# A four-layer graph network on one core: the third layer's weight product as Strassen's seven half-size products over pairs of tiles

## The reference

```python
h = relu(layernorm(x))                     # layer 3, a graph convolution
deg = segment_sum(ones, dst) + 1           # self loops
dinv = 1 / sqrt(deg)
out = segment_sum((h @ W)[src] * (dinv[src] * dinv[dst]), dst) + b
x = x + relu(out)
h = relu(layernorm(x))                     # layer 4, attention
h = h @ W4
...
```

## Time and profile before

| | |
|---|---|
| runs | 986.07, 985.63, 986.05 us; median 986.05 |
| the profiled execution's span | 985.7 us, 0.35 below the median of the runs |
| TensorE matmul / weight load busy | 968.1 us (98%) / 805.6 us (82%) |
| VectorE / ScalarE / GpSimd busy | 664.2 (67%) / 468.8 (48%) / 138.7 us (14%) |
| layer three's product on TensorE | from 613.70 us to 723.40 us of the span |

### The profile page before, as it was taken

The page is one execution under the profiler, slowest core; times in us unless marked ns, Lnnn a source line. Parts: engine busy times, 40 slices in busy tenths (PEclk is TensorE's granted clock), DMA queues, the critical chain, the costliest instruction groups (busy, mean ns, idle before and its releaser), DMA issues.

```text
span 985.7 us, 14150 instructions
## 1 busy us (share of the span) xinstructions
PE 968.1 (98%) x5199; PEld 805.6 (82%) x5200; DVE 664.2 (67%) x1193; ACT 468.8 (48%) x719; POOL 138.7 (14%) x191
## 2 busy tenths in 40 slices
PE   4999999999999999999999999999999999999998
PEld 3888878888888888888888888888888888888887
DVE  6987798788788779378884115333346664967777
ACT  5778864554554547223335446001012232766654
POOL 3022400000000001223331000010000000333331
PEclk9999999999999999999999999999999999999999
DMA  6256490000000005543422040733232130201222
GB/s 237 104 191 228 129 268 1 1 23 0 0 21 0 0 0 118 103 147 125 141 93 65 1 172 8 280 118 107 86 128 70 69 122 1 86 20 66 85 85 81
DMA packets 26006, 88.29 MB, mean 90 GB/s; under 512 B 3384, under 2 KB 3580, under 8 KB 25808
## 3 DMA queue, kind: packets, MB, share of 16 engines
q1 hardware_dynamic: 15072, 52.82, 14.8%
q0 software_dynamic: 10880, 34.74, 11.6%
HBM read 59.23 MB, written 33.56 MB: 94 GB/s over the span
## 4 chain that ended last, share of the span: by engine, by line
PE 95%; DVE 1%; ACT 1%; POOL 1%; DMA 1%; issue 0%; SPq 0%; ACTq 0%; DVEq 0%; POOLq 0%
PE ps L615 22%; PE ps L2271 13%; PE ps L2245 11%; PE ps L2165 9%; PE ps L2166 9%; PE ps L2167 9%; PE ps L2221 5%; PE ps L2217 5%; PE ps L598 3%; PE ps L2088 2%; PE ps L2090 1%; PE ps L2089 1%; PE ps L2013 1%; PE ps L2016 1%; PE ps L2057 1%; PE ps L2282 1%
## 5 line engine op out<-in xcount | busy, mean ns | idle before, releaser
L2165 PE MATMUL ps<-g_hi,mask_hi 128*128 128x512 f32 x400 | 157.7, 394 | 0.2 <-DVE mask_lo L1628 0.2
L2167 PE MATMUL ps<-g_hi,mask_lo 128*128 128x512 f32 x400 | 155.9, 390 | 0.0
L2166 PE MATMUL ps<-g_lo,mask_hi 128*128 128x512 f32 x400 | 155.8, 389 | 0.0
L1144 ACT ACTIVATE mask<-ps,v 128x640 f32<-128x640 f32 x80 | 63.2, 793 | 95.7 <-PE ps L2167 49.1
L2271 PE MATMUL ps<-y_all,att_hi 128*128 128x512 f32 x380 | 103.6, 392 | 0.0
L2165 PEld LDWEIGHTS ps<-g_hi,mask_hi 128*128 128x128 f32 x400 | 75.1, 188 | 19.0 <-DVE mask_lo L1628 2.3
L581 ACT ACTIVATE hT_hi<-ps 128x1024 fp32r<-128x1024 f32 x30 | 30.8, 1026 | 123.6 <-PE ps L598 123.4
L2167 PEld LDWEIGHTS ps<-g_hi,mask_lo 128*128 128x128 f32 x400 | 75.1, 188 | 16.0
L2166 PEld LDWEIGHTS ps<-g_lo,mask_hi 128*128 128x128 f32 x400 | 75.1, 188 | 14.8
L615 PE MATMUL ps<-w,hT_hi 128*128 128x512 f32 x320 | 86.6, 392 | 0.0
L2271 PEld LDWEIGHTS ps<-y_all,att_hi 128*128 128x128 f32 x380 | 70.4, 188 | 14.8 <-issue 0.4
(11 more groups left out here) (232 smaller groups left out, 1968.3 us busy)
## 6 DMA issues: line engine op xcount, KB each, us to landing
xin<-x_after SPq DMA_DIRECT2D x20, 512.0 KB, 3.2
xres<-x_after POOLq DMA_DIRECT2D x20, 512.0 KB, 3.6
x_after<-xres POOLq DMA_DIRECT2D x20, 512.0 KB, 2.9
w_raw<-in_L_gnn_W SPq DMA_DIRECT2D x8, 1024.0 KB, 9.8
x_after<-g POOLq DMA_DIRECT2D x20, 256.0 KB, 7.6
xin<-in_x SPq DMA_DIRECT2D x9, 512.0 KB, 3.5
x_after<-in_x SPq DMA_DIRECT2D x8, 512.0 KB, 5.2
weight_rows<-weight_row POOLq DMA_DIRECT2D x8, 512.0 KB, 3.8
```

The lines of the kernel that those rows point to most:

```text
L1144: nc.scalar.activation(mask[k][:, :], U_ALL, ACT.Tanh, bias=v[:, s:s + 1]).then_inc(tanh_ready, 1)
L2165: nc.tensor.matmul(SUMS[dd], mask_hi[k][:, cols], g_hi[:, s, :], start=(s == 0), stop=False)
L2166: nc.tensor.matmul(SUMS[dd], mask_hi[k][:, cols], g_lo[:, s, :], start=False, stop=False)
L2167: last = nc.tensor.matmul(SUMS[dd], mask_lo[k][:, cols], g_hi[:, s, :], start=False, stop=(s == T - 1))
```

## The change

What is a loop over ten tiles becomes 35 units (`UNITS`). Tile `t` (0 to 4) and tile `t + 5` form a pair of block rows, the two halves of the contraction and of the output columns the other blocks. Strassen's scheme (in Winograd's form) makes the four result blocks of a pair from seven products of half size: `A11`, `A12`, `S2`, `S1`, `S4`, `S3`, `A22` are the left factors, each with its own right factor (`B11`, `B21`, `T2`, `T1`, `B22`, `T3`, `T4`). A unit is one such product: four blocks of the contraction, three matmuls each, 12 matmuls of 128 x 512 in one PSUM bank. Units of one kind stand together for the five pairs, in that order; the last ten alternate (S3 0, S3 1, A22 0, S3 2, A22 1, ...), and an `A22` accumulates on the bank of its pair's `S3`.

- After a pass VectorE alone takes the sums out, times `dis` (`take_pass`), as plain 32-bit numbers.
- GpSimd forms the left block sums (`add_block`, 20 of them) and adds the bias to five partial sums (`bias_second`), 26 adds of 128 x 512 with that of the bias itself. VectorE forms the right ones (`w2_sum`) during the fourth pass.
- Each unit's left factor is split anew: high part by ScalarE (`part_hi_of`), low part by VectorE (`part_lo_of`), three units ahead, in six buffers. The right factors are split when their room is free (`SPLIT_AT`).
- For each unit VectorE adds the bank to a running sum (`take_unit`). For the 20 units that end a result block ScalarE takes relu (`relu_of`), and GpSimd issues a DMA that accumulates the block on `x` in DRAM (`add_unit`), in place of load, add and store.
- The fourth layer's weights are loaded once units 19 and 24 are done, and split in units 25 to 34 (`W3_AT`).
- Small edits follow: `dis` is stored and read back as a row, semaphores are shared, a loop of SP is written out.

The diff, cut to its core; behind the tables come the programs of GpSimd, ScalarE, VectorE and TensorE, in this order:

```diff
+UNITS = ([("A11", t, B11) for t in range(PAIRS)] + [("A12", t, B21) for t in range(PAIRS)] + [("S2", t, T2) for t in range(PAIRS)]
+         + [("S1", t, T1) for t in range(PAIRS)] + [("S4", t, B22) for t in range(PAIRS)]
+         + [unit for n in range(PAIRS + 1) for unit in ([("S3", n, T3)] if n < PAIRS else []) + ([("A22", n - 1, T4)] if n > 0 else [])])
+UNIT_BANKS = (0, 1, 6, 7, 0, 1, 6, 7, 0, 1, 2, 3, 4, 5, 2, 3, 4, 5, 2, 3, 0, 1, 4, 5, 0)
+LATE_BANKS = (1, 2, 3, 0, 1)
+SPLIT_AT = {0: (T2, 0), 1: (T2, 1), 3: (T1, 0), 4: (T1, 1), 6: (B22, 0), 7: (B22, 1), 11: (T3, 0), 12: (T3, 1), 16: (T4, 0), 17: (T4, 1)}
+RELU_UNITS = [n for n, (kind, _, _) in enumerate(UNITS) if kind in ("A12", "S4", "S3", "A22")]
+W3_AT = {25: 0, 26: 1, 27: 2, 28: 3, 30: 4, 31: 5, 33: 6, 34: 7}
...
-        pool.wait_ge(cnt_used, T * len(PASSES))
-        load2(0, 0)
...
+        for kind in ("S1", "S2"):
+            for t in range(PAIRS):
+                add_block(kind, t)
+        for t in range(PAIRS):
+            add_block("S4", t)
+            add_unit(t)
+        for t in range(PAIRS):
+            add_block("S3", t)
+            bias_second(t)
+        for m in range(PAIRS, len(RELU_UNITS)):
+            add_unit(m)
...
-        for k in range(KT):
-            act.wait_ge(product_ready[k % 2], dense[2].pairs(k // 2 + 1))
-            split_act(act, dense[3], [k])
-            if k == KT - 3:
-                h_act(act, dense[3], 0, 0)
-                h_act(act, dense[3], 0, 1)
-        transposed_act(act, dense[3], 0, 0)
-        root_act(act, dense[3], 0)
+        for n in range(len(UNITS) + 1):
+            if n + BLOCK_LEAD < len(UNITS):
+                part_hi_of(n + BLOCK_LEAD)
+            if n in SPLIT_AT:
+                w2_hi_of(*SPLIT_AT[n])
+            if n - 1 in RELU_UNITS:
+                relu_of(n - 1)
+            if n in W3_AT:
+                split3_act(W3_AT[n])
+            if n in (len(UNITS) - 4, len(UNITS) - 3):
+                h_act(act, dense[2], 0, n - (len(UNITS) - 4))
+            if n == len(UNITS) - 1:
+                transposed_act(act, dense[2], 0, 0)
+                root_act(act, dense[2], 0)
...
+        def take_unit(n):
+
+            kind, t, _ = UNITS[n]
+            dve.wait_ge(unit_done, n + 1)
...
+            if kind == "A12" and t >= len(top_left):
+                dve.wait_ge(half_stored[t - len(top_left)], 48)
...
+            nc.vector.tensor_tensor(unit_sum(n), UNIT_BANK[n], other, ALU.add).then_inc(unit_read, 1)
...
+        for n in range(len(UNITS) + 1):
+            if n + BLOCK_LEAD < len(UNITS):
+                part_lo_of(n + BLOCK_LEAD)
...
+            if n > 0:
+                take_unit(n - 1)
+            if n in SPLIT_AT:
+                w2_lo_of(*SPLIT_AT[n])
+            if n in W3_AT:
+                split_dve(dve, dense[2], [W3_AT[n]])
+            if n in (28, 29):
+                stats_dve(dve, dense[2], 0, n - 28)
...
+            if n == len(UNITS) - 1:
...
+                transposed_dve(dve, dense[2], 0, 0)
+        scale_dve(dve, dense[2], 0)
...
+        def unit_pe(n):
+
+            kind, t, w = UNITS[n]
+            pe.wait_ge(part_lo_ready, n + 1)
+            pe.wait_ge(w2_lo_ready, 2 * w + 2)
+            users = [m for m in range(n) if BANK_OF[m] == BANK_OF[n]]
+            if users:
+                pe.wait_ge(unit_read, users[-1] + 1)
...
+            for k in range(QK):
+                if k == QK // 2 and n == len(UNITS) - 1:
+                    transpose_pe(pe, dense[2], 0, 0)
...
```

More of the change, by code:

```diff
@@ L133, in build_program @@
     wt_lo = at("wt_lo", [P, KT, D], F32R, R_W + 32 * KIB)
[L134 to L137, removed]
+    w3_raw = [at(f"w3_raw{n}", [P, KT // 2, D], F32, place) for n, place in enumerate((R_Y + 48 * KIB, R_Y))]
     w3 = at("w3", [P, KT, 2, D], F32R, R_W)
@@ L663, in dense_act, with sums_place @@
         finish(HT - 1, 1)
-    def sums_place(p, pair, part):
+    def sums_place(p, pair):
         f, c = PASSES[p]
[L668 to L671, removed]
+        tiles = slice(PASS_TILES * c, min(PASS_TILES * (c + 1), T))
+        return sums[:, tiles, QK * f + 2 * pair:QK * f + 2 * pair + 2, :].rearrange("p t k n -> p k t n")
     def sums_bank(p, pair):
@@ L787, in _ @@
         load_x3(1)
-        sp.wait_ge(w_lo_ready, KT * 4)
-        with sp.Fori(2, HT) as i:
+        sp.wait_ge(w_lo_ready, KT * 3)
+        for i in range(2, HT):
             load_x3(i)
@@ new lines, in bias_second, with add_unit @@
+        def bias_second(t):
+            pool.wait_ge(unit_read, UNIT_OF["S1", t] + 1)
+            pool.wait_ge(add_done, 1)
+            nc.gpsimd.tensor_tensor(second_sum[:, t, :], second_sum[:, t, :], row_all[:, HID:D], ALU.add).then_inc(add_done, 1)
+        def add_unit(m):
+            kind, t, _ = UNITS[RELU_UNITS[m]]
+            pool.wait_ge(relu_done, m + 1)
+            tile = t if kind in ("A12", "S4") else PAIRS + t
+            half = 0 if kind in ("A12", "A22") else 1
+            pool.dma_start(x3_dram[tile * P:(tile + 1) * P, half * HID:(half + 1) * HID], unit_sum(RELU_UNITS[m]), accum_op=ALU.add
+                           ).then_inc(half_stored[t] if tile < PAIRS else bottom_added, 16)
@@ L939, in _ @@
+        pool.wait_ge(unit_done, len(UNITS))
         for b in range(2):
[L940 to L943, removed]
             pool.dma_start(att_all[b][:, :], att[0, b * D:(b + 1) * D].partition_broadcast(P)).then_inc(att_landed, 16)
@@ L2251, in _ @@
-        for t in range(T):
-            gcn_product(t)
+        def unit_pe(n):
[5 more added lines that the diff above has]
+                pe.wait_ge(unit_read, users[-1] + 1)
+            elif BANK_OF[n] in (2, 3, 4, 5):
+                pe.wait_ge(sums_read, 2 * len(PASSES))
+            else:
+                pe.wait_ge(sums_read, 2 * len(PASSES) - 2)
+            of = parts[n % BLOCK_RING]
+            for k in range(QK):
+                if k == QK // 2 and n == len(UNITS) - 1:
+                    transpose_pe(pe, dense[2], 0, 0)
+                for left, rights in ((of[:, 0, k, :], (W2_HI[w], W2_LO[w])), (of[:, 1, k, :], (W2_HI[w],))):
+                    for right in rights:
+                        last = nc.tensor.matmul(UNIT_BANK[n], left, right[:, k, :],
+                                                start=(kind != "A22" and k == 0 and len(rights) == 2 and right is W2_HI[w]),
+                                                stop=(k == QK - 1 and len(rights) == 1), skip_group_check=True)
+            last.then_inc(unit_done, 1)
@@ L2255, in spread_al @@
+        for n in range(len(UNITS)):
+            unit_pe(n)
         def spread_al(tiles):
```

379 lines of the change are left out of this document (252 added, 127 removed).

## The result

The changed kernel takes 996.66 us, the median of four runs (995.65 to 997.86), against 985.92 for the kernel before beside it: 1.0108 times as long (95% interval 1.0095 to 1.0121), 10.7 us slower. The forecast was 984.3, no change.

The account below looks back on a forecast made before the run. TensorE's matmul count times spacing was taken to bound the kernel; 13.6 - 0.7 - 11.2 left 1.7 us less, 985.7 to 984.0, or 984.3 with 0.35 for runs. Range 982.8 to 986; with rivals 981.5 to 992.

Parts of the forecast that it names:

- The gain of 13.6: In layer three's weight product, 60 matmuls fewer at 0.2267 us each: 13.6 us less.
- Units 25 to 34, the ring, 11.2 lost: In units 25 to 34 ScalarE and VectorE hand over in a cycle 1.4 us too slow, 11.2 us lost.
- 107.9: Forecast start of layer four's product, in us after the sums' end.
- the seam: Between the last unit and layer four's product, transposes and their two copies: 1 to 1.5 us lost.
- Units 0 to 9, 0.7 lost: GpSimd's first ten adds alternate with VectorE's two-SBUF-input instructions, so unit 8's take comes late: 0.7 us lost.
- rival 2: GpSimd keeps the port through its ten adds, units 0 to 9; unit 3 waits 8.3 us: 991.9 us; 18% with variants.
- that the port costs nothing behind unit 8: After unit 8, GpSimd's adds beside VectorE's low parts: the forecast counted no loss.
- my reading of rows 13: An add waited until VectorE was done, then had its turn before VectorE's next instruction; turns go by arrival.
- the fourth to sixth pass: at nothing: Twelve VectorE instructions for the right factors, 14 us in a stage where it idles for two thirds, cost nothing.
- rival 1: TensorE falls to half speed after its 4.9 us wait before layer four's product: 2.3 us more, 986.6; chance 20%.
- At nothing: the accumulating transfers: Unit 9's take reuses a buffer whose accumulating transfer lands with 2 us to spare: no cost.
- The 0.35 between span and run: The runs' median was taken as 0.35 us above the profiled span, turning 984.0 into 984.3 us.

Follow-up runs that it names:

- experiment 8: The changed kernel with layer-three loads later, S4 adds later, split ahead of relu, rows ahead of weights, and GpSimd's adds on 2 columns: 974.14 us.
- experiment 3: The changed kernel with GpSimd's S4 adds 1 to 4 waiting until VectorE's low part is done: 989.32 us.
- experiment 1: The changed kernel with the last three loads of layer three's weights waiting until the second pass is over: 992.54 us.
- Experiment 6: The changed kernel with 17 matmuls on zeros filling TensorE's wait before layer four's product: 993.21 us.
- experiments 4 and 5: 4: block split ahead of the relu, against the changed kernel, 990.04 us; 5: the same and rows loaded ahead of the last weights, 984.68 us.

## Why the prediction was wrong

- *The gain of 13.6* held: the units' matmuls are 0.227 apart, 420 of them, and with nothing else in the way the stage is 97.4 us (experiment 8).
- *Units 25 to 34, the ring, 11.2 lost*: right, in mechanism and size. 4.11 was forecast from take to take, 4.08 measured; with the port's trouble removed (experiment 3) the waits are 2.59, 1.40, 1.08 and 4.51 for 3.2, 1.7, 1.4 and 4.9, and the stage 108.19 for 107.9. That is 97.4, 1.6 at units 5 to 8 and 9.2 of ring; with the seam's 1.3 the ring's term is 10.5.
- *Units 0 to 9, 0.7 lost*: the add was 1.29 as taken and the wait before unit 8 came, 1.1 with the restart; with the little ones before units 5 to 7 it is 1.6 (experiment 8). The engines took turns in the row of ten, so rival 2 did not happen as written.
- **The step that failed first: that the port costs nothing behind unit 8.** I followed the ten S1 and S2 adds, and set none of the S4 adds against the low parts of units 10 to 13. Each add stands behind a DMA issue that waits for a relu, and behind the same relu ScalarE makes the high part that the next low part waits for, so they meet every time; and my reading of rows 13, that the one who comes first has the turn, did not hold there. Removed, it gives back 6.1 us (experiment 3), half speed in unit 31 among it. This was the slower rival's cause, the port, at another place.
- **The second: "the fourth to sixth pass: at nothing"**, where I counted VectorE's instructions and not the transfers for them. The loads, issued 13 us into the passes, stopped TensorE (through a late fetch of instructions, as far as the packets tell): 3.6 us in the profiled run, 2.0 of pause with its restart (92.44 - 90.48) and 1.6 of half speed (94.08 - 92.44). With the loads later it is nothing (experiment 1).
- **The third: the clock**, rival 1, was there at two places, and a third time behind the pause: 1.7 us in layer four's product (2.3 were priced; 1.3 to 2.2 in the other profiles with this wait), 1.5 in unit 31 (eight matmuls in 3.31 us). Experiment 6 shows for the product that the idle time is what brings it.
- *"At nothing: the accumulating transfers"*: right, no take waited for one. But the weights made the rows of layer four's first pair, which the prediction doesn't mention, land in 14.9 us; the ring hid that (experiments 4 and 5).
- The 0.35 between span and run was an accident of a single profile. The runs of before that gave both numbers lie 1.5 above their span, those after 1.7.

The sum by its own terms: 984.3 + 6.4 (units: 114.28 for 107.9) + 3.6 + 1.7 is 996.0, for 996.7 measured; what is left is that last point, 1.4, less 0.65 by which the passes started earlier.

## What to carry to other kernels

Where two engines hand work to and fro inside one unit's time, lay the whole cycle out: an instruction that needs nothing from the cycle (a weight split) belongs ahead of the one that waits, not behind it. For every add put on GpSimd, ask which VectorE instruction with two SBUF inputs the same event releases; a wait that starts the add behind that one cost nothing here and gave back 6 us with what followed from it. Large loads had two victims here: smaller loads queued behind them (16.2 us in place of 6.3), and TensorE, which waits for none of them and stopped all the same when they came at one place of its program. Issued 7 us later they no longer did.

## What the runs showed that I had not expected

- One instruction fetch, 2.3 to 3.2 us later behind 3 MB of loads, went with a stop of TensorE of 1.65 to 1.79 us in five profiles of five.
- GpSimd's add, recorded 0.35 to 0.38 us behind VectorE's low part and with a DMA issue of its own ahead of it, went first all four times. DMA issues of GpSimd without an add behind them (689.13, 691.64) left the low parts beside them at 0.69. Why the later one wins stays open. The Trainium skill ("SBUF — State Buffer", "Who interferes with whom") gives the shared port to the one that issues first; by the starts that the profile records, these four pairs do not agree. Its other half, that an instruction with one SBUF input goes free, does: takes are 0.68 beside adds everywhere.
- The fall to half speed is not settled by the length of the idle time alone. In the three stages it came after 1.65 to 1.79 us in two of five profiled runs, after 2.59 once not, after 2.80 and more always, and after 1.40 and less never. Full speed was back 3.0 to 4.7 us after TensorE resumed. What decides between 1.65 and 2.6 was not tried.
